# Channel order, DRAM layout and transfers of the query and key stacks in a four-layer kernel on one core

## The chip, the cores and the metric

The kernel runs on one core of one Trainium2 chip. The metric is the device time of one execution in microseconds (us), here the median of three runs. The engines are TensorE (PE), VectorE (DVE), ScalarE (ACT), GpSimd (POOL) and SyncE (SP). Every transfer in this kernel is issued by SP, and 16 DMA engines carry them.

## The reference

`x` has shape 8 x 512 x 128: eight batches of 512 tokens with 128 channels. Four layers follow each other, and each has the form `x = x + attn(xn) * act(ffn(xn))`, where `xn` is the layer norm of `x`. Layer 0 attends in a band of 32 tokens, layer 2 is linear attention. What is changed touches layers 1 and 3:

```python
# layer 1: causal attention, 8 heads of 8 channels, on the first 64 channels ("local"),
# and on 128 compressed tokens ("global")
lq, lk, lv = jnp.split(local_x @ w_lqkv + b_lqkv, 3, axis=-1)
local_out = _causal_attn(_split_heads(lq, Tx), _split_heads(lk, Tx), _split_heads(lv, Tx))
gq, gk, gv = jnp.split(cg @ w_gqkv + b_gqkv, 3, axis=-1)
# layer 3: attention without a mask, 16 heads of 8 channels, 512 tokens
q = jnp.einsum('btd,hdk->bhtk', hidden_states, Wq) + bq[None, :, None, :]
k = jnp.einsum('btd,hdk->bhtk', hidden_states, Wk) + bk[None, :, None, :]
scores = jnp.einsum('bhtk,bhsk->bhts', q, k) * scale
```

## The kernel before

**Two threads.** The work on a batch is cut in two programs. Thread A does layers 0 and 1, thread B does layers 2 and 3 with the mixtures of experts of layers 1 to 3. In turn n, thread A works on batch n and thread B on batch n-1, so turn 0 holds A alone, turns 1 to 7 hold both, and turn 8 holds B alone. Each engine executes its instructions in one fixed order. That order is woven when the program is written: each thread is a Python generator with one `yield` before each stretch of instructions, the table `STARTS` holds one number for each `yield`, and `weave` always continues the thread whose next number is lower, with `TURN` added for each further batch. The numbers only set the order of the instructions on each engine (SP's queue too). They set no time: what an engine waits for is written as semaphore waits. An engine whose next instruction waits does nothing of the other thread meanwhile.

**The stacks.** Queries and keys are computed channel by channel (`F3`, 128 partitions: 16 heads of 8 channels, and `FL`, `FG`, 64 partitions: 8 heads of 8). VectorE splits each value into three bf16 parts (`dve_split`, lines 1017 to 1020), so `SPL3` and `SPL` hold, for each channel, three parts of 512 tokens, and `SPLG` three parts of 128. A score is then a product over a stack of 72 partitions (9 pairs of a query part and a key part with 8 channels each), with 3 more partitions for ones and the row maximum. To bring 8 channels x 3 parts of every head under each other, the parts go through DRAM. `stack_out` stores them, with one transfer for each part: 3 for the queries and 5 for the keys (types 0, 1, 2, 0, 1). `stack_in` loads them as three blocks of 24 partitions, for the queries three times the same block, for the keys shifted by one type (`HD` rows) each time. So one stack takes 8 stores and 6 loads. In DRAM the order is head, type, channel, token, and each contiguous run is 512 tokens of bf16, 1 KB (256 B of it in the global part). There are three stacks for each batch: local and global in thread A (`QSL`, `KSL`, `QSG`, `KSG`) and that of layer 3 in thread B (`QS3`, `KS3`).

**What follows the stacks.** In thread B, TensorE computes 32 pairs of score tiles (line 1720), VectorE takes their maxima (line 1568), negates and splits them (lines 1572 to 1576), TensorE turns them (line 1731), ScalarE copies them (line 1426), three small transfers put them in `QS3` (line 1327), and 64 scores are computed again the other way round (line 1753), with ScalarE's exponential (line 1434) and the products with the values (line 1742). In thread A, the same is done for layer 1 (scores in line 1194).

**What lies beside them.** While thread B is at the stack of layer 3, thread A is at the end of the band attention of layer 0: ScalarE's exponential (line 786), four stores of the weights in runs of 128 B with a skew (`band_scratch`, line 658), four loads of the bands (line 664), products with the values (line 1126), the sums of the weights (line 1134), VectorE's reciprocal and product (lines 934, 935) and the projection (line 1140). All these transfers are on SP's queue, as are the stacks' ones and the weights of the expert pairs (`WST`, `GW`).

Of the kernel before, what the change touches and what calls it, by code (L numbers as in the profile page):

```python
# [1945 lines left out]
```

## Time and profile before

| What | Value |
|---|---|
| Median of the runs | 3959.35 us (3958.97 to 3961.12) |
| The profiled execution | 3941.28 us |
| Its span, first to last instruction | 3939.5 us |
| Granted TensorE clock, mean | 0.864 |
| PE busy | 3131.8 us, 79% of the span |
| DVE busy | 2503.1 us, 64% |
| ACT busy | 1661.7 us, 42% |
| POOL busy | 689.7 us, 18% |
| DMA | 330.82 MB in 332,142 packets, mean 84 GB/s |

The profile is of one execution, which took 18.07 us less than the median. The shares are means over stages that differ much: in the stage of the stacks most engines stand idle for some 10 us, and in the expert stages TensorE is busy nearly all the time. A granted clock of 1.00 is 2.4 GHz and one of 0.50 is 1.2 GHz.

### The profile page before, as it was taken

The page shows a single profiled execution, that of the slowest core. Times are in us where ns is not written, and L with a number is a line of the kernel's source. Part 1 is how long each engine was busy: PE and PEld are TensorE (multiplying, and loading weights), DVE is VectorE, ACT ScalarE, POOL GpSimd, SP SyncE. Part 2 cuts the span into 40 slices and gives each one's busy share as a digit, 9 for nine tenths or more (in the row PEclk, how much of TensorE's full clock was granted, in tenths as well). Part 3 has the DMA queues.
Part 4 walks back from the last instruction along what each step waited for, and adds up shares of the span by engine and source line. Part 5 has one row for each costly group of instructions (what it writes and reads, how often), then busy time and mean ns, then how long its engine had stood idle before and what let it go on. Part 6 is the DMA issues. An engine that isn't in the chain of part 4 may idle for free.

```text
span 3939.5 us, 43890 instructions
## 1 busy us (share of the span) xinstructions
PE 3131.8 (79%) x16174; PEld 1566.9 (40%) x16174; DVE 2503.1 (64%) x4568; ACT 1661.7 (42%) x2458; POOL 689.7 (18%) x465
## 2 busy tenths in 40 slices
PE   4458768987799778997699868997689867996588
PEld 1124323553245333553245432553235432454145
DVE  5534876578656876669755776568765786534542
ACT  3415515464344524464154534455154643431241
POOL 2001201311023101312013110322013110211030
PEclk8568879997799879998699978998799987997696
DMA  2330174302741164301842055501743027411261
GB/s 90 36 97 31 31 133 119 105 8 79 122 138 55 23 118 122 116 16 43 144 131 76 1 106 103 157 29 32 132 121 103 7 78 122 135 57 43 58 193 48
DMA packets 332142, 330.82 MB, mean 84 GB/s; under 512 B 101448, under 2 KB 267144, under 8 KB 331656
## 3 DMA queue, kind: packets, MB, share of 16 engines
q1 hardware_dynamic: 331928, 328.01, 34.8%
q8 instruction: 128, 2.10, 0.2%
q14 instruction: 86, 0.70, 0.1%
HBM read 278.88 MB, written 47.78 MB: 83 GB/s over the span
## 4 chain that ended last, share of the span: by engine, by line
PE 55%; DVE 23%; DMA 7%; ACT 5%; SPq 4%; issue 4%; POOL 2%; ACTq 0%; DVEq 0%; POOLq 0%
PE PS L1774 6%; PE PS L1797 6%; PE PS L1628 5%; PE PS L1801 5%; PE PS L1636 5%; DMA U<-band_scratch 4%; PE PS L1075 4%; PE PS L1742 3%; DVE MX L1568 3%; SPq L658 3%; PE PS L1753 3%; DVE U L885 2%; DVE XN L558 2%; DVE U L878 2%; DVE D L1619 2%
## 5 line engine op out<-in xcount | busy, mean ns | idle before, releaser
L1380 POOL TENSOR_TENSOR D<-D,GW 128x512 f32<-128x512 f32 x320 | 429.5, 1343 | 1419.1 <-ACT D L1453 1190.9
L770 ACT ACTIVATE U<-U 128x2048 f32<-128x2048 f32 x256 | 488.7, 1909 | 188.6 <-DVE U L878 104.4
L1614 DVE SCALAR_TENSOR_TENSOR D<-D,PS 128x512 f32<-128x512 f32 x336 | 228.9, 681 | 400.9 <-ACT D L1457 283.6
L1453 ACT ACTIVATE D<-PS 128x512 f32<-128x512 f32 x336 | 200.1, 595 | 615.9 <-PE PS L1797 615.9
L1774 PEld LDWEIGHTS PS<-WST,D 128*128 128x128 f32 (+1 forms) x2688 | 350.4, 197 | 163.9 <-DVE D L1619 99.7
L1774 PE MATMUL PS<-WST,D 128*128 128x128 f32 (+1 forms) x2688 | 378.5, 285 | 31.6 <-DVE D L1619 31.5
L1801 PE MATMUL PS<-XT,WST 128*128 128x512 f32 (+1 forms) x672 | 373.4, 638 | 28.8 <-DVE D L1614 27.8
L1075 PE MATMUL PS<-U,resident 128*32 128x512 f32 x2048 | 306.1, 678 | 112.1 <-ACT U L770 112.1
L885 DVE SCALAR_TENSOR_TENSOR U<-PP,RD,QB 128x512 f32<-128x512 f32 x512 | 361.7, 771 | 46.4 <-ACT QB L767 27.6
L1568 DVE TENSOR_REDUCE MX<-PS 128x2 f32<-128x1024 f32 x256 | 299.5, 1220 | 121.9 <-PE PS L1720 121.8
L1797 PE MATMUL PS<-XT,WST 128*128 128x512 f32 (+1 forms) x672 | 366.6, 628 | 9.8 <-DMA WST<-in_pairs_dram 6.5
L1720 PE MATMUL PS<-UU 128*128 128x512 bf16 x512 | 220.8, 536 | 138.6 <-DMA UU<-k_scratch 83.2
L1434 ACT ACTIVATE D<-PS 128x512 f32<-128x512 f32 x512 | 269.0, 604 | 119.1 <-PE PS L1753 119.0
L878 DVE TENSOR_TENSOR U<-EP,QE 128x2048 f32<-128x2048 f32 x128 | 306.2, 2409 | 16.0 <-PE PS L1075 15.2
L1636 PEld LDWEIGHTS PS<-UU,D 128*128 128x128 f32 x2048 | 264.4, 191 | 121.5 <-issue 115.5
L1619 DVE TENSOR_TENSOR D<-D 128x512 f32<-128x512 f32 x336 | 252.1, 750 | 38.8 <-POOL D L1380 31.5
L1628 PE MATMUL PS<-XT,UU 128*128 128x512 f32 x512 | 269.7, 614 | 0.9 <-DVE GB L1587 0.9
L1636 PE MATMUL PS<-UU,D 128*128 128x128 f32 x2048 | 269.3, 276 | 0.0
L1393 ACT ACTIVATE D<-PS,resident 128x512 f32<-128x512 f32 x256 | 173.6, 684 | 144.6 <-PE PS L1628 144.0
L562 POOL TENSOR_TENSOR RS<-VE,half 128x4 f32<-128x4 f32 x32 | 46.1, 1441 | 993.0 <-DVE VE L554 993.0
L1753 PE MATMUL PS<-UU 128*128 128x512 bf16 x512 | 164.6, 406 | 46.1 <-DMA UU<-NMT 33.3
L1457 ACT ACTIVATE D<-PS 128x512 f32<-128x512 f32 x336 | 199.7, 594 | 0.0
(350 smaller groups left out, 4035.4 us busy)
## 6 DMA issues: line engine op xcount, KB each, us to landing
GW<-gates_scratch SPq DMA_DIRECT2D x320, 256.0 KB, 4.2
WST<-in_pairs_dram SPq DMA_DIRECT2D x336, 192.0 KB, 2.4
U<-band_scratch SPq DMA_DIRECT2D x32, 1280.0 KB, 14.9
UU<-in_w_dram SPq DMA_DIRECT2D x64, 512.0 KB, 7.4
UU<-q_scratch SPq DMA_DIRECT2D x24, 384.0 KB
UU<-k_scratch SPq DMA_DIRECT2D x24, 384.0 KB
e_scratch<-D SPq DMA_DIRECT2D x8, 1024.0 KB, 4.5
D<-e_scratch SPq DMA_DIRECT2D x32, 256.0 KB, 3.9
```

Source lines behind the costliest of these rows:

```text
L770: e.activation(ring(i), ring(i), ACT.Gelu).then_inc(S["act"], 1)
L878: last = e.tensor_tensor(ring(i).rearrange("p (q t) -> p q t", q=4), win, QE[:, h, :].unsqueeze(1).broadcast_to([P, 4, T]), ALU.add)
L885: last = e.scalar_tensor_tensor(out=ring(i)[:, T * x:T * x + T], in0=PP[:, h, PAD - o:PAD - o + T], scalar=RD[:, HOR - 1 - o:HOR - o], in1 ...
L1075: last = e.matmul(PS(L0_BANK[g, kind])[32 * q:32 * q + 32, :], wout[:, 1 - kind, c, :], ring(i)[:, T * x:T * x + T], start=(c == 0), stop= ...
L1380: e.tensor_tensor(AV[:, n % 3, :], AV[:, n % 3, :], GW[:, p // 2 % GWS, p % 2, :], ALU.mult).then_inc(S["gated"], 1)
L1568: e.tensor_reduce(MX3[:, j:j + 2, hd], PSall[:, 4 + j:6 + j, :], AX.X, ALU.max).then_inc(S["max3"], 1)
L1619: e.tensor_tensor(AV[0:m, n % 3, :], AV[0:m, n % 3, :], SL[0:m, n % 3, :], ALU.mult).then_inc(S["av"], 1)
L1628: e.matmul(PZ(f % 2), w1slot(x)[:, 0, P * f:P * f + P], XT(b), start=True, stop=True).then_inc(S["h1_ps"], 1)
L1636: last = e.matmul(PZ(2 + x % 2)[:, P * j:P * j + P], HB[:, x % 2, f, P * j:P * j + P], w1slot(x)[:, 1, P * f:P * f + P], start=(j == 0 and ...
L1774: last = e.matmul(PZ(3)[:, P * j:P * j + P], AV[0:m, n % 3, P * j:P * j + P], WST[0:m, (PAIRS * b + n) % WS, 2, :], start=(p == 0 and j == ...
L1797: e.matmul(PZ(0)[0:m, :], w[:, 0, 0:m], XT(b), start=True, stop=True).then_inc(S["u_ps"], 1)
L1801: e.matmul(PZ(1)[0:m, :], w[:, 1, 0:m], XT(b), start=True, stop=True).then_inc(S["v2_ps"], 1)
```

## The change

The channels of the queries and keys are reordered on the host from head, dimension to dimension, head (`by_dim`), in the weights and the biases. A partition of `SPL3` is then a pair of dimension and head, and the DRAM arrays become two-dimensional: a row for each type and dimension, and in the row all heads' tokens in a row, 16 KB for layer 3, 8 KB for the local stack and 2 KB for the global one. One store now writes all three parts of the queries, one the first three types of the keys, one the last two. The stacks are filled by two loads each: one for the first 48 partitions, and one for the last 24. What is stored and what stands in the stacks in the end is as many bytes as before.

```diff
-        ql_dram = nc.dram_tensor("ql_scratch", (NH // 2, 3, HD, T), BF16).ap()
+        ql_dram = nc.dram_tensor("ql_scratch", (3 * HD, NH // 2 * T), BF16).ap()
...
-        k3_dram = nc.dram_tensor("k3_scratch", (NH, 5, HD, T), BF16).ap()
+        k3_dram = nc.dram_tensor("k3_scratch", (5 * HD, NH * T), BF16).ap()
...
         def stack_out(e, spl, nh, n, qd, kd, q_sem, k_sem):
-            for k in range(3):
-                dst = bass.AP(qd.tensor, k * HD * T, [[3 * HD * T, nh], [T, HD], [1, n]])
-                e.dma_start(dst, spl[0:8 * nh, 0, k, 0:n]).then_inc(S[q_sem], 16)
-            for k in range(5):
-                dst = bass.AP(kd.tensor, k * HD * T, [[5 * HD * T, nh], [T, HD], [1, n]])
-                e.dma_start(dst, spl[0:8 * nh, 1, KTYPES[k], 0:n]).then_inc(S[k_sem], 16)
-
-        def stack_in(e, stack, rows, shift, nh, n, dram, signal):
-
-            for r in range(3):
-                e.dma_start(stack[24 * r:24 * r + 24, 0:nh, 0:n], bass.AP(dram.tensor, r * shift * T, [[T, 24], [rows * T, nh], [1, n]])).then_inc(S[signal], 16)
+            e.dma_start(bass.AP(qd.tensor, 0, [[n, 8 * nh], [8 * nh * n, 3], [1, n]]), spl[0:8 * nh, 0, :, 0:n]).then_inc(S[q_sem], 16)
+            for k0, k1 in ((0, 3), (3, 5)):
+                dst = bass.AP(kd.tensor, k0 * 8 * nh * n, [[n, 8 * nh], [8 * nh * n, k1 - k0], [1, n]])
+                e.dma_start(dst, spl[0:8 * nh, 1, 0:k1 - k0, 0:n]).then_inc(S[k_sem], 16)
+
+        def stack_in(e, stack, shift, nh, n, dram, signal):
+
+            for r0, r1 in ((0, 2), (2, 3)):
+                src = bass.AP(dram.tensor, r0 * shift * nh * n, [[shift * nh * n, r1 - r0], [nh * n, 24], [1, nh * n]])
+                e.dma_start(stack[24 * r0:24 * r1, 0:nh * n], src).then_inc(S[signal], 16)
```

The first pair in an access pattern is its slowest dimension: a step and a count. The waits follow the numbers of transfers (`q_out3` from 48 to 16, `k_out3` from 80 to 32, `stacked3` from 96 to 64, and so on).

Second, chains of VectorE instructions get a `yield` between their steps, so that the other thread's instructions may come in between: `dve_split`, `dve_kept`, `dve_gates`, `dve_update`, the splitting of the maxima, parts of layer 2 and of the mixing. The instructions are the same but for one: the reciprocal of line 934 is cut into two of 512 elements.

```diff
             e.wait_ge(S["den"], at("den", b, 1))
-            step(e, e.reciprocal(RCA[:, :, :], PSall[:, 2:4, :]))
+            for h in range(2):
+                last = e.reciprocal(RCA[:, h, :], PS(2 + h))
+                if h == 0:
+                    yield
+            step(e, last)
+            yield
             e.tensor_tensor(OS[:, :, :], OS[:, :, :], RCA[:, :, :], ALU.mult).then_inc(S["on"], 1)
...
         def dve_split(e, f, part, signal):
             step(e, e.tensor_copy(part(0), f))
+            yield
             step(e, e.tensor_tensor(f, f, part(0), ALU.subtract))
+            yield
             step(e, e.tensor_copy(part(1), f))
+            yield
             e.tensor_tensor(part(2), f, part(1), ALU.subtract).then_inc(S[signal], 1)
```

Third, `TURN` and all of `STARTS` are new. The lines of the table in which the end of the band attention meets thread B's scores:

```diff
-TURN = 429.40
+TURN = 423.40
...
     "a_dve": (
-        181.59, 182.54, 184.12, 188.61, 192.04, 194.85, 209.94, 212.88, 264.22, 274.87, 275.50, 277.88, 280.62, 287.54, 291.47, 300.89,
+        179.49, 180.44, 182.02, 186.51, 189.93, 190.58, 192.75, 192.97, 207.85, 210.79, 262.47, 262.91, 263.47, 266.13, 266.76, 267.63,
...
     "a_pe": (
-        183.40, 183.46, 184.85, 186.75, 198.54, 211.08, 213.25, 214.20, 215.14, 216.09, 244.09, 249.11, 254.26, 259.70, 262.09, 272.76,
+        181.30, 181.35, 182.74, 184.63, 196.45, 208.98, 209.93, 210.88, 211.83, 212.78, 242.37, 247.34, 252.30, 258.11, 260.34, 264.02,
...
     "b_pe": (
-        264.01, 268.48, 268.73, 268.97, 269.61, 270.11, 270.60, 271.10, 272.05, 272.29, 272.52, 274.66, 274.89, 275.84, 276.08, 276.32,
+        259.55, 265.92, 266.17, 266.41, 267.05, 267.55, 268.04, 268.54, 269.49, 269.73, 269.96, 270.58, 271.08, 272.03, 272.27, 272.50,
```

Which `yield` a number belongs to follows from the code. In `a_pe` the last six numbers of the line are the four band products (line 1126), the sums (line 1134) and the projection (line 1140). In `b_pe` the first two are the transposes of the maxima (line 1731) and the first score of line 1753; the last of the 32 score pairs (line 1720) stands at 260.65 before and at 253.49 after. In `a_dve`, 264.22 is the reciprocal with its product and 274.87 the addition behind the projection before; after, these are 262.47 and 262.91 (the two reciprocals), 263.47 (the product) and 266.13.

## Rows read from the trace of the kernel before

**Rows 1.** The page, section 4: the chain that ended last, by line.

```profile
PE PS L1774 6%; PE PS L1797 6%; PE PS L1628 5%; PE PS L1801 5%; PE PS L1636 5%; DMA U<-band_scratch 4%; PE PS L1075 4%; PE PS L1742 3%; DVE MX L1568 3%; SPq L658 3%; PE PS L1753 3%; DVE U L885 2%; DVE XN L558 2%; DVE U L878 2%; DVE D L1619 2%
```

**Rows 2.** Timeline of SyncE: start us, length us, where X is saved in turns 1 and 7.

```profile
510.17 0.33 SPq L1311 DMA_DIRECT2D x_scratch<-X  x1
...
3227.39 0.33 SPq L1311 DMA_DIRECT2D x_scratch<-X  x1
```

**Rows 3.** Timeline of SyncE in turn 4: start us, length us, issue.

```profile
1881.52 1.85 SPq L702 DMA_DIRECT2D q_scratch<-D  x3
...
1886.63 1.57 SPq L710 DMA_DIRECT2D UU<-q_scratch  x3
...
1893.40 17.35 SPq L658 DMA_DIRECT2D band_scratch<-D  x4
1910.79 20.36 SPq L664 DMA_DIRECT2D U<-band_scratch  x4
...
1979.54 1.96 SPq L702 DMA_DIRECT2D ql_scratch<-D  x3
```

**Rows 4.** Timeline of TensorE in turn 4: start us, length us; in brackets the idle time before.

```profile
1903.76 1.89 PE L1720 MATMUL PS<-UU 128*128 128x512 bf16 x4 [8.53 <-DMA UU<-k_scratch]
...
1927.22 2.36 PE L1126 MATMUL PS<-U,VP 128*32 128x160 f32 x32 [1.23 <-DMA U<-band_scratch]
...
1944.76 1.08 PE L1126 MATMUL PS<-U,VP 128*32 128x128 f32 x32
...
1947.08 1.96 PE L1134 MATMUL PS<-QE,consts 128*128 128x512 f32 x4
1951.69 0.40 PE L1731 MATMUL PS<-identb,NM 128*48 128x128 bf16 x4 [2.65 <-DVE NM L1576]
1956.19 2.94 PE L1753 MATMUL PS<-UU 128*128 128x512 bf16 x6 [4.10 <-DMA UU<-NMT]
...
1961.34 1.95 PE L1140 MATMUL PS<-resident,QE 128*128 128x128 f32 x16
...
2004.08 0.22 PE L1194 MATMUL PS<-U 128*128 128x128 bf16 x1
```

**Rows 5.** Timeline of VectorE in turn 4.

```profile
1904.84 22.43 DVE L1568 TENSOR_REDUCE MX<-PS 128x2 f32<-128x1024 f32 x19 [11.28 <-PE PS L1720]
...
1941.81 5.83 DVE L1568 TENSOR_REDUCE MX<-PS 128x2 f32<-128x1024 f32 x5 [0.20 <-PE PS L1720]
...
1951.55 6.55 DVE L934 RECIPROCAL D<-PS 128x1024 f32<-128x1024 f32 x1
1958.13 1.23 DVE L935 TENSOR_TENSOR QE<-QE,D 128x1024 f32<-128x1024 f32 x1
```

**Rows 6.** Timeline of SyncE in turn 8, where thread B runs alone.

```profile
3646.32 1.87 SPq L702 DMA_DIRECT2D q_scratch<-D  x3
...
3652.27 1.57 SPq L710 DMA_DIRECT2D UU<-q_scratch  x3
```

**Rows 7.** Timeline of TensorE in turn 8.

```profile
3668.51 1.89 PE L1720 MATMUL PS<-UU 128*128 128x512 bf16 x4 [24.32 <-DMA UU<-k_scratch]
```

**Rows 8.** Timeline of VectorE in turn 8.

```profile
3669.58 37.40 DVE L1568 TENSOR_REDUCE MX<-PS 128x2 f32<-128x1024 f32 x32 [12.84 <-PE PS L1720]
```

**Rows 9.** Windows: stretch, length, busy us by engine, TensorE clock, DMA share, GB/s.

```profile
3660.00:3662.00 2.00, 0.00 (x0) 0.00 (x0) 0.00 (x0) 0.00 (x0) 0.00 (x0) 0.50 0.83 169
...
252.00:253.00 1.00, 1.00 (x2) 0.34 (x1) 0.00 (x0) 0.58 (x1) 0.00 (x0) 0.50 0.40 102
...
3635.00:3636.00 1.00, 0.00 (x0) 0.00 (x0) 0.96 (x4) 0.00 (x0) 0.00 (x0) 0.50 0.10 19
...
2019.00:2021.00 2.00, 0.77 (x5) 0.25 (x3) 2.00 (x2) 1.08 (x2) 1.00 (x1) 1.00 1.03 410
```

**Rows 10.** Timeline of SyncE in turn 0, where thread A runs alone.

```profile
250.66 1.89 SPq L702 DMA_DIRECT2D ql_scratch<-D  x3
```

**Rows 11.** Timeline of TensorE in turn 0.

```profile
265.05 0.29 PE L1194 MATMUL PS<-U 128*128 128x128 bf16 x1 [3.99 <-DMA U<-kl_scratch]
```

More of the change, by code:

```diff
@@ L91, in laid_out, with by_dim @@
     beside = lambda v, n: np.asarray(v).reshape(n, P, -1).transpose(1, 0, 2).reshape(P, -1)
+    def by_dim(w):
+        w = np.asarray(w)
+        return w.reshape(w.shape[:-1] + (-1, HD)).swapaxes(-1, -2).reshape(w.shape)
     def per_head(w):
@@ L112, in laid_out @@
     bc[:, 36:38] = w("L0_attn_b_disp").reshape(2, P).T
-    bc[:, 38] = w("L3_attn_bq").reshape(-1)
-    bc[:, 39] = w("L3_attn_bk").reshape(-1)
+    bc[:, 38] = by_dim(w("L3_attn_bq").reshape(-1))
+    bc[:, 39] = by_dim(w("L3_attn_bk").reshape(-1))
     for k, n in ((40, "L1_attn_b_lqkv"), (42, "L1_attn_b_gqkv")):
-        bc[0:LD, k] = w(n)[0:LD]
-        bc[0:LD, k + 1] = w(n)[LD:2 * LD]
+        bc[0:LD, k] = by_dim(w(n)[0:LD])
+        bc[0:LD, k + 1] = by_dim(w(n)[LD:2 * LD])
     bc[0:LD, 44] = w("L1_attn_b_comp")[LD:C]
@@ L131, in laid_out @@
     v["lu"] = w("L0_ffn_lora_up").transpose(0, 2, 1).reshape(P, C)
-    v["wqkv1"] = np.concatenate([w("L1_attn_w_lqkv"), w("L1_attn_w_gqkv")], 1)
+    v["wqkv1"] = np.concatenate([f(w(n)[:, LD * k:LD * k + LD]) for n in ("L1_attn_w_lqkv", "L1_attn_w_gqkv")
+                                 for k, f in enumerate((by_dim, by_dim, np.asarray))], 1)
     v["wcomp"] = beside(w("L1_attn_w_comp"), R1).reshape(P, R1, C)[:, :, LD:].reshape(P, -1)
@@ L141, in laid_out @@
     v["b_out"] = rows(w("L2_attn_b_out"))
-    v["wqkv3"] = np.concatenate([w(f"L3_attn_{n}").transpose(1, 0, 2).reshape(C, P) for n in ("Wq", "Wk", "Wv")], 1)
+    v["wqkv3"] = np.concatenate([w(f"L3_attn_{n}").transpose(1, *o).reshape(C, P) for n, o in (("Wq", (2, 0)), ("Wk", (2, 0)), ("Wv", (0, 2)))], 1)
     v["bv"], v["gate_bias"] = rows(w("L3_attn_bv")), rows(w("L3_ffn_gate_bias"))
@@ L285 @@
     "band_used": 4, "f0_ps": 4, "f0_sb": 2, "a_f": 1, "a_t": 1, "a_x": 1, "a_best_dif": 2, "a_best_exp": 2,
-    "qk_ps": 2, "qk": 4, "v_ps": 2, "v": 2, "split": 2, "q_out": 48, "k_out": 80, "split_out_g": 128, "stacked": 96, "stacked_g": 96,
+    "qk_ps": 2, "qk": 4, "v_ps": 2, "v": 2, "split": 2, "q_out": 16, "k_out": 32, "split_out_g": 48, "stacked": 64, "stacked_g": 64,
     "zero_a": 3, "ones_a": 32, "s1": 40, "max": 40, "nm": 1, "nm_t": 1, "nmt": 1, "nm_in": 96, "s2": 40, "p": 40, "pv": 10,
@@ L672, in a_sp @@
             yield
[L673 to L674 removed]
+            e.wait_ge(S["q_out"], at("q_out", b, 16))
+            stack_in(e, UB[:, 0:8 * T], 0, 8, T, ql_dram, "stacked")
             yield
[L676 to L677 removed]
+            e.wait_ge(S["k_out"], at("k_out", b, 32))
+            stack_in(e, UB[:, 8 * T:16 * T], HD, 8, T, kl_dram, "stacked")
             yield
@@ L917, in a_dve @@
             dve_best(e, A8[:, 1], A8[:, 0], A8[:, 2], A8[:, 3], 1, 1, 8, 2, "a_best_dif")
-            dve_kept(e, A8[:, 1], A8[:, 0], A8[:, 2], 1, 1, 8, 2)
+            yield from dve_kept(e, A8[:, 1], A8[:, 0], A8[:, 2], 1, 1, 8, 2)
             yield
             e.wait_ge(S["a_best_exp"], at("a_best_exp", b, 1))
-            step(e, dve_gates(e, A8[:, 3], A8[:, 2], A8[:, 4], AS, 1, 1, 8))
+            step(e, (yield from dve_gates(e, A8[:, 3], A8[:, 2], A8[:, 4], AS, 1, 1, 8)))
             e.tensor_copy(GX[0:1, :].rearrange("p (e r) -> p e r", e=8), A8[0:1, 4, 0, 0:8].unsqueeze(2).broadcast_to([1, 8, 16])).then_inc(S["f0_sb"], 1)
@@ L933, in a_dve @@
             e.wait_ge(S["den"], at("den", b, 1))
-            step(e, e.reciprocal(RCA[:, :, :], PSall[:, 2:4, :]))
+            for h in range(2):
[3 more added lines that the diff above has]
+            step(e, last)
+            yield
             e.tensor_tensor(OS[:, :, :], OS[:, :, :], RCA[:, :, :], ALU.mult).then_inc(S["on"], 1)
@@ L940, in a_dve @@
             e.wait_ge(S["a_t"], at("a_t", b, 1))
-            dve_update(e, b, 0.5).then_inc(S["a_x"], 1)
+            (yield from dve_update(e, b, 0.5)).then_inc(S["a_x"], 1)
             e.wait_ge(S["a_x"], at("a_x", b, 1))
@@ L945, in a_dve @@
             e.wait_ge(S["qk"], at("qk", b, 2))
-            dve_split(e, FL[0:64, :, :], lambda k: SPL[0:64, :, k, :], "split")
+            yield from dve_split(e, FL[0:64, :, :], lambda k: SPL[0:64, :, k, :], "split")
             yield
@@ L951, in a_dve @@
             e.wait_ge(S["qk"], at("qk", b, 4))
-            dve_split(e, FG[0:64, :, 0:P], lambda k: SPLG[0:64, :, k, :], "split")
+            yield from dve_split(e, FG[0:64, :, 0:P], lambda k: SPLG[0:64, :, k, :], "split")
             yield
@@ L960, in a_dve @@
             dve_best(e, A8[:, 1], A8[:, 0], A8[:, 2], A8[:, 3], P, NT, E1, 2, "a_best_dif")
-            dve_kept(e, A8[:, 1], A8[:, 0], A8[:, 2], P, NT, E1, 2)
+            yield
+            yield from dve_kept(e, A8[:, 1], A8[:, 0], A8[:, 2], P, NT, E1, 2)
             yield
             e.wait_ge(S["a_best_exp"], at("a_best_exp", b, 2))
-            dve_gates(e, A8[:, 3], A8[:, 2], GT1(b), AS, P, NT, E1).then_inc(S["g1"], 1)
+            (yield from dve_gates(e, A8[:, 3], A8[:, 2], GT1(b), AS, P, NT, E1)).then_inc(S["g1"], 1)
             e.wait_ge(S["g1"], at("g1", b, 2))
@@ L978, in a_dve @@
             step(e, last)
+            yield
             for v in both:
@@ L984, in a_dve @@
             step(e, last)
+            yield
             for v in both:
@@ L993, in a_dve @@
             e.reciprocal(RCA[:, 1, 0:P], PS(1)[:, 0:P])
+            yield
             step(e, e.reciprocal(RCA[:, 0, :], PS(0)))
+            yield
             each = lambda v: v.unsqueeze(2).broadcast_to([P, P, R1])
@@ L1003, in a_dve @@
             e.wait_ge(S["mix"], at("mix", b, 2))
+            yield
             step(e, e.tensor_tensor(SB(b), LO(b), over(WDIF[:, 0:C]), ALU.mult))
+            yield
             step(e, e.tensor_reduce(AS[:, :], SB(b), AX.X, ALU.add))
@@ L1017, in dve_split @@
             step(e, e.tensor_copy(part(0), f))
+            yield
             step(e, e.tensor_tensor(f, f, part(0), ALU.subtract))
+            yield
             step(e, e.tensor_copy(part(1), f))
+            yield
             e.tensor_tensor(part(2), f, part(1), ALU.subtract).then_inc(S[signal], 1)
@@ L1476, in b_dve @@
             e.wait_ge(S["b_t"], at("b_t", b, 1))
-            dve_update(e, b, 0.5).then_inc(S["b_x"], 1)
+            (yield from dve_update(e, b, 0.5)).then_inc(S["b_x"], 1)
             e.wait_ge(S["b_x"], at("b_x", b, 1))
@@ L1483, in b_dve @@
             step(e, e.tensor_scalar(KV[:, :, 0, :], ps[:, :, 0, :], 0.0, EPS2, ALU.max, ALU.add))
+            yield
             e.tensor_copy(KV[:, :, 1, :], ps[:, :, 1, :]).then_inc(S["l2_dve"], 1)
+            yield
             e.tensor_scalar(HT(b), PZ(1), 0.0, EPS2, ALU.max, ALU.add).then_inc(S["l2_dve"], 1)
@@ L1501, in b_dve @@
             step(e, e.reciprocal(SM[:, :], SM[:, :]))
+            yield
             for j in range(NT):
@@ L1504, in b_dve @@
             last.then_inc(S["l2_dve"], 1)
-            dve_kept(e, SCO, M8, RPL, P, NT, E2, K2)
+            yield
+            yield from dve_kept(e, SCO, M8, RPL, P, NT, E2, K2)
             yield
@@ L1508, in b_dve @@
             e.wait_ge(S["gate_act"], at("gate_act", b, 1))
-            dve_gates(e, DIF, RPL, GT, SM, P, NT, E2).then_inc(S["gate_dve"], 1)
+            (yield from dve_gates(e, DIF, RPL, GT, SM, P, NT, E2)).then_inc(S["gate_dve"], 1)
             yield from b_dve_pairs(e, b, 2)
@@ L1514, in b_dve @@
             e.wait_ge(S["b_t"], at("b_t", b, 2))
-            dve_update(e, b, 1.0).then_inc(S["b_x"], 1)
+            (yield from dve_update(e, b, 1.0)).then_inc(S["b_x"], 1)
             e.wait_ge(S["b_x"], at("b_x", b, 2))
@@ L1519, in b_dve @@
             e.wait_ge(S["qk3"], at("qk3", b, 2))
-            dve_split(e, F3[:, :, :], lambda k: SPL3[:, :, k, :], "split3")
+            yield from dve_split(e, F3[:, :, :], lambda k: SPL3[:, :, k, :], "split3")
             yield
@@ L1572, in b_dve @@
             step(e, e.tensor_scalar(f, MX3[:, :, :], -1.0, None, ALU.mult))
+            yield
             step(e, e.tensor_copy(part(0), f))
             step(e, e.tensor_tensor(f, f, part(0), ALU.subtract))
+            yield
             step(e, e.tensor_copy(part(1), f))
@@ L1602, in b_dve_pairs @@
                     e.tensor_tensor(OS3[:, :, :], OS3[:, :, :], RC, ALU.mult).then_inc(S["nrm3"], 1)
+                    yield
                     e.wait_ge(S["nrm3"], at("nrm3", b, 3))
```

39 lines of the change are left out of this document (17 added, 22 removed), and 167 rows, old and new, of tables (PER, STARTS).

## The prediction

> **What bounds the kernel now.** I read the page first, then the chain of waits, then the timelines engine by engine around the stacks. The chain runs through many lines with single-digit shares, most of them TensorE's, but `U<-band_scratch` (DMA) and line 658 (SP's queue) stand among them with 4% and 3% [rows 1]. So the kernel is a sequence of stages with different limits. A joint turn lasts (3227.39 - 510.17) / 6 = 452.9 us [rows 2], and there are seven of them.
>
> The stage in question, in turn 4: the first store of the stack of layer 3 is issued at 1881.52, the first load at 1886.63, and then SP waits for the band weights and stores them from 1893.40 [rows 3]. TensorE starts the scores at 1903.76, after 8.53 us of waiting for the key load [rows 4], so 22.2 us lie between first store and first score. Then VectorE's maxima set the pace, from 1904.84 to 1941.81 + 5.83 = 1947.64, or 42.8 us [rows 5]. Band products stand between them and wait for their loads (1927.22 to 1944.76, the first and the last of four) [rows 4]. The reader is to see that two chains run side by side here, the stack with its maxima and the bands, and that both must end before line 1753 starts at 1956.19. In turn 8 the stack is alone: 3646.32 to 3668.51 is again 22.2 us [rows 6, 7], and the 32 maxima take only 37.40 [rows 8].
>
> **The loads.** What a DMA reaches depends on how many of the 16 engines carry it. The windows show it [rows 9]: a store whose slow dimension on the DRAM side is 8 (local stack) keeps a share of 0.40 busy. The loads with 24 partitions stand at 0.83, with 169 GB/s, long after the last was issued. The fill of three partitions shows 0.10 and 19 GB/s. Loads over 128 partitions reach 1.03 and 410 GB/s. The share follows the smaller of the counts in the slowest dimension, and 0.83 against 1.03 is some 12 or 13 of 16 engines. In the new load of 48 partitions the source's slowest dimension has a count of 2. By this series it runs on two engines, and the 24-row load on as many as now.
>
> The Trainium skill says the same as a rule (DMA: Bandwidth & Descriptors, "Why a DMA increments its semaphore by 16 and not by 1"): the number of engines is the largest up to 16 that divides the slowest counts of both sides. For 48 against 2 it gives 2, and for 24 it gives 12; the shares above agree. The same page's "Rules for kernel authors" advises joining small transfers into large ones, which speaks for this change; the sum below goes by the shares.
>
> Rate of one engine: 410 / (16 x 1.03) = 24.9 GB/s with long runs. The other end is today's stack load, 169 / 12 = 14.1 GB/s with 1 KB runs. I take 24.9, because runs grow to 16 KB and two engines fall short of today's total by far.
>
> Layer 3, each of queries and keys: 48 rows of 16,384 B over two engines are 24 x 16,384 / 24.9 = 15.8 us; the third block, two rows for each of 12 engines, adds 1.3. Together 2 x 17.1 = 34.2 us. The first load is issued 5.1 us after the first store now [rows 3]; with one store for the queries that is between one issue (0.6) and 5.1, and I take 4. Start and landing add 2.2: in turn 8 the six loads, 2.36 MB at 169 GB/s or 14.0 us, took 3668.51 - 3652.27 = 16.2. First store to first score: 4 + 34.2 + 2.2 = 40.4 us against 22.2, so **+18.2 us**. At 14.1 GB/s it would be +44. On 16 engines the loads would take 2.36 MB / 398 GB/s = 5.9, in all 12.1, so -10.1.
>
> **Turn 8:** no cover, +18.2. **Turn 0:** the local stack, 250.66 to 265.05, takes 14.4 us [rows 10, 11]. After: 4 + 2 x (24 x 8,192 B / 24.9 = 7.9, and 0.7) + 2.2 = 23.4, so +9.0.
>
> **Joint turns, layer 3.** Scores start at 1881.52 + 40.4 = 1921.9. The bands: engines 0 and 1 are free at about first store + 38; the band stores took 17.4 us and the loads 20.4 [rows 3], so the first band is there at about + 60 and the last at + 77. The new table puts the first band behind about 23 score pairs, at 40.4 + 27 = 67, and the last two behind all of them, at 78: just hidden. The maxima then end at 1921.9 + 1.1 + 37.4 = 1960.4 against 1947.64: **+12.8 us**, as the band waits (5.4 us) fall away.
>
> **Joint turns, the table.** Before, the sums (line 1134) run ahead of the transposes (line 1731), and the reciprocal fills the time in which the maxima travel [rows 4, 5]. The new table has transposes 259.55, sums 260.34, projection 264.02, first score 265.92. Between the first reciprocal and the addition behind the projection it leaves 266.13 - 262.47 = 3.7 us, where the row has 6.55 for the reciprocal alone [rows 5]. TensorE keeps its order, so the first score of line 1753 now waits for sums 1.96, reciprocals 6.55, product about 1.2 and projection 1.95: 0.6 + 1.96 + 6.55 + 1.3 + 1.95 = 12.4 us after the maxima are split, against 1956.19 - 1951.6 = 4.6 now. Of these 7.8 us, 1.95 is work that leaves the later stretch. **+5.8 us.** Behind it stand all of thread B's scores, ScalarE's exponentials and the expert pairs.
>
> **Joint turns, local stack.** From projection to thread A's first score are 42.7 us now, without a wait [rows 4]; the table cuts this distance from 39.46 to 35.95, or about 38.9 in real time. The chain needs 1979.54 - 1961.34 = 18.2 to the first store [rows 3, 4], and then 23.4: 41.6. **+2 us**, between 0 and 5. The global stack (2 KB runs) is needed 24 us later in the table and lands in time.
>
> **What costs nothing or helps a little.** The `yield`s add no instruction. Two reciprocals in place of one add at most 0.1 us. Eight issues of about 0.6 us each become three; SP waits for the band weights until 1893.40 anyway [rows 3], so that frees nothing there. The channel order changes no matmul shape. `TURN` is 6.0 us shorter, and of that the two steps above are just what the plan got wrong; I credit 1 us for the rest, between 0 and 6.
>
> **The sum.** 7 x (12.8 + 5.8 + 2 - 1) = 137.2, and with 18.2 + 9.0 it is 164.4. Profiled execution: 3941.3 + 164.4 = 4105.7; the median of before lies 18.1 above its profiled one, so **4124 us**, 4% slower.
>
> **Rivals.** (1) *The loads spread over 12 or more engines after all* (the other side). For it: the transfers of the other lines with long runs reach 410 GB/s [rows 9]. Against it: every row whose slow count is below 16. Turn 8 gains between 2.0 us (4 + 14.0 + 2.2, the loads as fast as now) and 10.1, turn 0 about 3. In joint turns the scores start early, but the last band at 1944.76 stands ahead of the transposes, then sums, reciprocal, product and projection: first score at about 1958.8 instead of 1956.2, less 1.95. So nothing is won there but what the rest of the table gives, 1 to 5 us. Time 3959 - 10 - 7 x 2 = 3935, range 3915 to 3951. It decides when the loads do their 94.8 us of engine time (2.36 MB at 24.9 GB/s) in less than 22.2 - 6.2 = 16.0 us, that is from 6 engines on.
>
> (2) *Two engines, at the slow rate or with the bands behind them.* The band transfers queue behind the stack on engines 0 and 1; if they take 10 us longer than I allow, or an engine gives 14 GB/s, each turn loses 10 to 30 us more: 4240 and above.
>
> (3) *Two engines, but hidden.* If the table's order leaves TensorE other work and the reciprocals fall under the late scores, only turn 8, turn 0 and some us of each turn stay: 3967 to 3990.
>
> **Chances and range.** Forecast (3990 to 4240): 0.75. Rival 2: 0.03. Rival 3: 0.05. No change, gains and the table's stall in balance: 0.05. Rival 1: 0.12. The range 3967 to 4240 holds the forecast and rival 3, 0.80. A measurement of this kernel can tell about 0.2% (8 us) from no change: slower 0.83, same 0.05, faster 0.12.
>
> **What would show it.** In the windows between the last stack load and the first score the DMA share should fall to about 2/16 = 0.12 with some 50 GB/s, where it is 0.83 and 169 now. Line 1720's wait for the key load in turn 8 should grow from 24.3 to about 42 us, and in joint turns the scores should start some 40 us after the first store. Line 1140 should show a wait for line 935 of some 8 us, and line 1753 should come behind it. In turn 0, line 1194 should wait about 12 us for the local stack, instead of 3.99. The prediction is wrong if these windows show a share above 0.5, if the band loads end far beyond the scores, or if the expert stages shift by themselves.

## The result and the profile after

The changed kernel takes 4119.46 us in the median of four runs (4116.41 to 4121.84), where the kernel before takes 3959.16 on the same chip. The ratio is 1.0401, 95% interval 1.0385 to 1.0418: 4% slower, 160.3 us by the medians. The prediction said 4124. The profiled execution took 4121.84 us, with a span of 4120.1 and a mean granted clock of 0.847.

The page, section 4, the chain that ended last, by engine and by line (after):

```profile
PE 46%; DVE 24%; DMA 14%; ACT 5%; issue 3%; another core or an unknown queue 3%; POOL 2%; SPq 2%; ACTq 0%; DVEq 0%; POOLq 0%
DMA UU<-k_scratch 7%; DVE MX L1597 6%; PE PS L1806 6%; PE PS L1829 6%; PE PS L1833 5%; PE PS L1660 5%; PE PS L1668 4%; DMA U<-kl_scratch 3%; PE PS L1100 3%; DVE U L888 3%; DVE U L895 2%; PE PS L1774 2%; DVE XN L565 2%; POOL D L1405 2%
```

The lines to compare with [rows 1] are the loads of the key stacks. Before, neither was among the lines shown there: the chain waited for each only once, for `UU<-k_scratch` 13.5 us in turn 8 and for `U<-kl_scratch` 7.0 us in turn 0. Now `UU<-k_scratch` (layer 3) leads it with 7%, and `U<-kl_scratch` (local) has 3%. The packets fell only from 332,142 to 296,780.

**Turn 8, the stack alone.** Two windows (after): in the first the last load is issued, at 3816.21, and in the second only the loads are left. The last three figures are granted clock, DMA share, GB/s:

```profile
3815.00:3820.00 5.00, 0.00 (x0) 0.00 (x0) 4.62 (x32) 0.00 (x0) 0.00 (x0) 0.50 0.58 124
3820.00:3830.00 10.00, 0.00 (x0) 0.00 (x0) 0.62 (x3) 0.00 (x0) 0.00 (x0) 0.50 0.12 50
```

In the second window and those behind it the share is 0.12 to 0.13, two engines of sixteen, where [rows 9] has 0.83 and 169 GB/s. That is 25 to 27 GB/s for each engine. The timeline of SyncE, turn 8 (after):

```profile
3810.27 0.37 SPq L711 DMA_DIRECT2D q_scratch<-D  x1
...
3816.21 1.09 SPq L720 DMA_DIRECT2D UU<-k_scratch  x2
```

and that of TensorE with its first score (after):

```profile
3851.50 1.49 PE L1752 MATMUL PS<-UU 128*128 128x512 bf16 x3 [43.28 <-DMA UU<-k_scratch]
```

From the first store to the first score are 3851.50 - 3810.27 = 41.2 us, where [rows 6, 7] give 22.2 and the prediction said 40.4. The waits, summed over the run (after; us in total, times, longest):

```profile
PE PS L1752 <- DMA UU<-k_scratch: 240.0, 8, 43.3
...
PE PS L1219 <- DMA U<-kl_scratch: 26.0, 8, 12.1
```

The first was 83.2 us in 8 with a longest of 24.3 before. The second is new but for turn 0, where it was 3.99 and is now 12.1.

**Turn 4, a joint turn.** The timeline of SyncE (after), which answers to [rows 3]:

```profile
1959.06 0.39 SPq L711 DMA_DIRECT2D q_scratch<-D  x1
...
1962.21 1.13 SPq L720 DMA_DIRECT2D UU<-q_scratch  x2
...
1970.94 35.95 SPq L669 DMA_DIRECT2D band_scratch<-D  x4
2006.94 21.14 SPq L675 DMA_DIRECT2D U<-band_scratch  x4
...
2075.52 0.61 SPq L711 DMA_DIRECT2D ql_scratch<-D  x1
```

The stores of the band weights take 35.95 us to issue, where they took 17.35. TensorE, the same turn (after), which answers to [rows 4]:

```profile
2000.35 1.49 PE L1752 MATMUL PS<-UU 128*128 128x512 bf16 x3 [28.41 <-DMA UU<-k_scratch]
...
2026.30 1.29 PE L1151 MATMUL PS<-U,VP 128*32 128x160 f32 x32
...
2038.22 1.08 PE L1151 MATMUL PS<-U,VP 128*32 128x128 f32 x32
2043.31 0.62 PE L1763 MATMUL PS<-identb,NM 128*48 128x128 bf16 x4 [4.00 <-DVE NM L1607]
2043.86 3.78 PE L1159 MATMUL PS<-QE,consts 128*128 128x512 f32 x4
2055.56 3.79 PE L1165 MATMUL PS<-resident,QE 128*128 128x128 f32 x16 [7.92 <-DVE QE L950]
2059.57 0.65 PE L1785 MATMUL PS<-UU 128*128 128x512 bf16 x2 [0.22 <-issue]
...
2098.61 0.23 PE L1219 MATMUL PS<-U 128*128 128x128 bf16 x1 [2.02 <-DMA U<-kl_scratch]
```

VectorE, the same turn (after), which answers to [rows 5]:

```profile
2001.02 26.95 DVE L1597 TENSOR_REDUCE MX<-PS 128x2 f32<-128x1024 f32 x23 [29.91 <-PE PS L1752]
...
2037.81 1.23 DVE L1597 TENSOR_REDUCE MX<-PS 128x2 f32<-128x1024 f32 x1 [0.20 <-PE PS L1752]
...
2043.03 0.23 DVE L1607 TENSOR_TENSOR NM<-NMF,NM 128x64 bf16<-128x64 f32 x1
2047.68 6.57 DVE L945 RECIPROCAL D<-PS 128x512 f32<-128x512 f32 x2 [4.42 <-PE PS L1159]
2054.28 1.23 DVE L950 TENSOR_TENSOR QE<-QE,D 128x1024 f32<-128x1024 f32 x1
```

Read together: the scores start 41.3 us after the first store (22.2 before), the maxima end at 80.0 (66.1 before), the maxima are split at 84.2 (70.1). Then TensorE makes the sums, waits 7.92 us for VectorE's reciprocal and product, makes the projection and only then starts line 1785, which was line 1753 before, at 100.5 (74.7 before). Thread A's first score follows at 139.6 (122.6 before).

The turns, from where X is saved in turn 1 to turn 7 (after, SyncE), beside [rows 2]:

```profile
518.05 0.33 SPq L1336 DMA_DIRECT2D x_scratch<-X  x1
...
3370.74 0.33 SPq L1336 DMA_DIRECT2D x_scratch<-X  x1
```

(3370.74 - 518.05) / 6 = 475.4 us for a joint turn, 22.6 more than before.

### The profile page after: what moved, and what is told of

It reads as the page before. It is cut to its first block, busy times and chain, and to the rows that moved or that the text cites. A ratio compares the mean times of both kernels' runs of the same rounds, so it can differ in the third digit from the quotient of the medians.

```text
span 4120.1 us, 43645 instructions
## 1 busy us (share of the span) xinstructions
PE 3107.6 (75%) x16089; PEld 1576.7 (38%) x16174; DVE 2504.3 (61%) x4576; ACT 1662.0 (40%) x2458; POOL 692.7 (17%) x465
## 4 chain that ended last, share of the span: by engine, by line
PE 46%; DVE 24%; DMA 14%; ACT 5%; issue 3%; another core or an unknown queue 3%; POOL 2%; SPq 2%; ACTq 0%; DVEq 0%; POOLq 0%
DMA UU<-k_scratch 7%; DVE MX L1597 6%; PE PS L1806 6%; PE PS L1829 6%; PE PS L1833 5%; PE PS L1660 5%; PE PS L1668 4%; DMA U<-kl_scratch 3%; PE PS L1100 3%; DVE U L888 3%; DVE U L895 2%; PE PS L1774 2%; DVE XN L565 2%; POOL D L1405 2%
## 5 line engine op out<-in xcount | busy, mean ns | idle before, releaser
L1752 PE MATMUL PS<-UU 128*128 128x512 bf16 x489 | 210.9, 529 | 302.9 <-DMA UU<-k_scratch 240.0
L1478 ACT ACTIVATE D<-PS 128x512 f32<-128x512 f32 x336 | 200.2, 596 | 579.9 <-PE PS L1829 579.1
L1459 ACT ACTIVATE D<-PS 128x512 f32<-128x512 f32 x512 | 270.4, 602 | 202.6 <-remote 116.8
L1752 PEld LDWEIGHTS PS<-UU 128*128 128x128 bf16 x512 | 33.4, 106 | 474.1 <-DMA UU<-k_scratch 238.8
```

What stands on the lines that cost most here:

```text
L1459: e.activation(PT3[:, k % 8, :], PZ(k % 3), ACT.Exp, scale=SCALE).then_inc(S["p3"], 1)
```

## Experiments on the loads

Each kernel has its ratio to the kernel before, timed beside it on the same chip. The kernel before took 3959.16 us beside the changed one, but 3976.72 to 3983.38 beside the experiments. So only ratios are compared across these groups, and, between profiles, the time since the first store of the stack. Microseconds for a difference of ratios are worked out on 3959.

**Three loads of 24 rows** (`e1_three_loads`): the change with only the joining of the first two blocks undone.

```diff
-            for r0, r1 in ((0, 2), (2, 3)):
+            for r0, r1 in ((0, 1), (1, 2), (2, 3)):
```

> The changed kernel with each stack filled by three loads of 24 rows instead of one of 48 and one of 24; rows stay 16, 8 and 2 KB, the table stays the new one. Theory 1 (a load runs on as many engines as its smaller slowest count allows): 24 rows run on about 12 engines, so 2.36 MB take some 8 us, first store to first score in turn 8 falls from 41.2 to 14 to 16 us, the DMA share meanwhile rises above 0.5, and the time falls by 130 to 180 us, to 3940 to 3990. Theory 2 (long rows into few partitions are slow by themselves, whatever the number of engines): the time stays within 20 us of 4119. Theory 3 (the new table is the cause): it stays too.

Measured: 3950.09 us against 3983.38, ratio 0.9916 (0.9891 to 0.994). One line (and the counts of the waits that go with it) makes 0.8% faster out of 4% slower, which is 192 us, a little more than the 130 to 180 expected. So the joined load is the cause of the loss. The first score was expected 14 to 16 us after the first store, and that was too early: it comes at 19.8. A window in turn 8 while the loads run (three loads):

```profile
3676.00:3680.00 4.00, 0.00 (x0) 0.00 (x0) 2.75 (x14) 0.00 (x0) 0.00 (x0) 0.50 0.68 147
```

TensorE's first score there, with the first store at 3668.56:

```profile
3688.33 1.89 PE L1752 MATMUL PS<-UU 128*128 128x512 bf16 x4 [21.71 <-DMA UU<-k_scratch]
```

In turn 4, SyncE issues the band stores in 16.79 us again, as before (three loads):

```profile
1899.34 0.38 SPq L711 DMA_DIRECT2D q_scratch<-D  x1
...
1911.23 16.79 SPq L669 DMA_DIRECT2D band_scratch<-D  x4
1928.07 23.67 SPq L675 DMA_DIRECT2D U<-band_scratch  x4
```

So the long issue of the band stores follows from the stack's loads. In turn 4 it ends 28.7 us after the first store here and 47.8 us in the change, and the first scores stand at 20.1 and 41.3: in every variant it ends 6 to 9 us after the first score. Whether SyncE is held up by the small number of engines, or only until the loads are through, these runs don't separate.

**One load of 72 rows** (`e8_one_load`): the slowest dimension of the source then has a count of 3.

```diff
-            for r0, r1 in ((0, 2), (2, 3)):
+            for r0, r1 in ((0, 3),):
```

> The changed kernel with one load of 72 rows per stack operand, whose source has a slowest count of 3. Theory 1: three engines of 24 rows each work side by side, DMA share about 3/16 = 0.19, 75 to 80 GB/s, and each operand takes 15.1 to 15.8 us instead of 17, so turn 8 gains about 3 us and the time falls by 10 to 30 us, to 4090 to 4110. Theory 2: the share stays at 0.12 and the time within 8 us of 4119, or it rises.

Measured: 4053.19 us, ratio 1.0176 (1.0153 to 1.0198). A window of turn 8 (one load):

```profile
3757.00:3762.00 5.00, 0.00 (x0) 0.00 (x0) 0.00 (x0) 0.00 (x0) 0.00 (x0) 0.50 0.18 79
```

A share of 0.18 is three engines, at 26 GB/s each, and the first score comes 34.7 us after the first store. The count was right and the size was not: against 1.0401 this gives back 2.2%, some 90 us, where I had expected 10 to 30. The first score gains 6.5 us in turn 8, where 3 were expected, and the gain grows on the way through a joint turn. In turn 4 the scores start 6.1 us earlier (35.2), the maxima end 6.0 earlier (74.0), line 1785 starts 11.0 earlier (89.5) and thread A's first score comes 12.8 earlier (126.8). Part of this is peculiar to that turn. The change (after), one step in the splitting of the maxima and GpSimd beside it:

```profile
2039.79 3.20 DVE L1606 CAST NM<-NMF 128x64 bf16<-128x64 f32 x1
...
2039.40 3.55 POOL L738 MEMSET U<- 128x4096 f32 x1 [92.56 <-PE PS L1151]
```

The same with one load, and TensorE behind it:

```profile
2005.48 0.20 DVE L1606 CAST NM<-NMF 128x64 bf16<-128x64 f32 x1
...
2005.63 3.51 POOL L738 MEMSET U<- 128x4096 f32 x1 [87.43 <-PE PS L1151]
...
2005.99 0.40 PE L1763 MATMUL PS<-identb,NM 128*48 128x128 bf16 x4 [0.45 <-DVE NM L1607]
2006.77 1.95 PE L1159 MATMUL PS<-QE,consts 128*128 128x512 f32 x4 [0.38 <-ACT QE L802]
```

In the change GpSimd's memset of line 738 started just ahead of the cast, and the cast ended 0.04 us after the memset. Here the cast came first and took 0.20 us. So TensorE waited 0.45 us for the maxima instead of 4.00, and ran the sums in 1.95 us instead of 3.78. In turns 1, 3, 6 and 7 the cast is slow here too (3.2 to 3.4 us), and line 1785 gains only 4.8 to 7.0 us. Averaged over the seven joint turns the maxima end 5.6 us earlier, thread A's first score comes 9.3 earlier, and a turn is 10 shorter. Of the 9.3, 2.0 are the wait for the local stack, which is gone in the joint turns: only turn 0 still waits for it, 9.5 us, where the change has 26.0 us in eight.

**48 contiguous rows** (`e2_flat48`): the DRAM arrays repeat the types (six for the queries, seven for the keys), so that the first load is 48 rows in one piece and both its slowest counts are 48. It costs two more stores.

```diff
...
-                src = bass.AP(dram.tensor, r0 * shift * nh * n, [[shift * nh * n, r1 - r0], [nh * n, 24], [1, nh * n]])
+                src = bass.AP(dram.tensor, (0 if r0 == 0 else 4 * shift) * nh * n, [[nh * n, rows], [1, nh * n]])
```

> The changed kernel with the DRAM arrays lengthened to 6 types of queries (0 1 2 0 1 2) and 7 of keys (0 1 2 1 2 0 1), so that the first 48 partitions are loaded from 48 rows that lie one after another: the same two loads per operand, the same rows of 16 KB, but a slowest count of 48 on both sides instead of 48 against 2. Five stores instead of three, 0.64 MB more. New table. Theory 1 (engines by slowest count): 16 and 12 engines, first store to first score 15 to 21 us instead of 41.2, time 3930 to 3990 where before is 3983. If the limit of about 165 GB/s that 24 rows on 12 engines show is one of the 24 target partitions, 48 partitions run near twice that and the score starts at 16 to 17 us; if it is one of these reads as a whole, at 20 to 21 us. Theory 2 (one load of 48 partitions with long rows is slow by itself): within 20 us of the changed kernel, 1.04 of before.

Measured: 3954.82 us against 3978.89, ratio 0.9936 (0.9915 to 0.9958). A window of turn 8 (48 contiguous rows):

```profile
3673.00:3677.00 4.00, 0.00 (x0) 0.00 (x0) 1.87 (x7) 0.00 (x0) 0.00 (x0) 0.50 0.91 143
```

The large transfer is harmless once its slowest count is 48: joining as such was not at fault. But 14 to 16 busy engines carry no more than twelve, 168 GB/s (in the window 3677 to 3683). The score comes at 22.1, no earlier than before, and a little behind the 20 to 21 that I expected if the reads as a whole are limited. With a limit set by the 24 target partitions it would have come at 16 to 17, so 48 partitions did not lift the limit. Part of the 22.1 are the two more stores: the first load is issued 3.9 us after the first store, with three loads 2.5. Against three loads, 0.9936 and 0.9916 are not apart beyond their intervals.

**Six and four rows** (`e10_six_rows`, `e11_four_rows`): the stack in 12 loads of 6 rows, or 18 of 4.

```diff
-            for r0, r1 in ((0, 2), (2, 3)):
...
+            for j in range(12):
+                src = bass.AP(dram.tensor, (j // 4 * shift + j % 4 * 6) * nh * n, [[nh * n, 6], [1, nh * n]])
+                e.dma_start(stack[6 * j:6 * j + 6, 0:nh * n], src).then_inc(S[signal], 16)
```

> The changed kernel with each stack loaded by twelve transfers of 6 rows (slow count 6 on both sides) instead of 48 + 24 rows. Engines follow the smaller slow count: 6 engines at the 26 to 28 GB/s that an engine showed when 2 or 3 carried the loads are 156 to 168 GB/s, which is what 12 engines reached (165). So the first score of the layer-3 stack comes 20 to 22 us after the first store, as with loads of 24 rows, 1 to 2 us later for 24 issues in place of 6; the loss is gone, 0.99 to 1.00 of before. If each engine gives only the 14 GB/s that it showed among 12, the loads take 28 us, the score comes at 34 and the kernel stands at 1.015 or above.

> The same with eighteen transfers of 4 rows. Engine-bound, 4 x 26 to 28 = 104 to 112 GB/s: 2.36 MB take 21 to 23 us, the first score comes 27 to 29 us after the first store (41.3 with two engines, 35.2 with three, 20.1 with twelve), and the kernel stands between those of three and twelve engines, 1.00 to 1.01 of before. At 14 GB/s for each engine it would be 42 us and the whole loss of the changed kernel, 1.04.

Measured: 3984.17 us (3965.49 to 4004.21 in ten runs) with six rows, ratio 1.0019 (1.0 to 1.0038), and 4022.95 with four, ratio 1.0104 (1.0076 to 1.0132). Windows of turn 8 (six rows):

```profile
3689.00:3693.00 4.00, 0.00 (x0) 0.00 (x0) 0.00 (x0) 0.00 (x0) 0.00 (x0) 0.50 0.37 98
3693.00:3697.00 4.00, 0.00 (x0) 0.00 (x0) 0.00 (x0) 0.00 (x0) 0.00 (x0) 0.50 0.40 109
```

and one with four rows:

```profile
3735.00:3740.00 5.00, 0.00 (x0) 0.00 (x0) 0.00 (x0) 0.00 (x0) 0.00 (x0) 0.50 0.27 108
```

The shares are right, 0.26 for four engines and 0.36 to 0.40 for six. The rates are not: four engines give 26 to 27 GB/s each, six only 16 to 18. Over the turns the first score comes 26 to 29 us after the first store with six rows, and 30 to 35 with four, later than the 20 to 22 and 27 to 29 that I expected, and both ratios lie at or just above the upper end of what I gave (1.00 and 1.01). So there is a second limit. Of all the variants, by the windows of turn 8:

| Slowest count | DMA share | GB/s | First store to first score, turn 8, us | Ratio to before |
|---|---|---|---|---|
| 2 (48 + 24 rows, the change) | 0.12 to 0.13 | 50 to 54 | 41.2 | 1.0401 |
| 3 (72 rows) | 0.18 | 79 | 34.7 | 1.0176 |
| 4 (4 rows) | 0.26 to 0.27 | 108 | 31.1 | 1.0104 |
| 6 (6 rows) | 0.36 to 0.40 | 98 to 109 | 29.4 | 1.0019 |
| 24 (24 rows) | 0.68 to 0.76 | 147 to 164 | 19.8 | 0.9916 |
| 48 and 24 | 0.89 | 168 | 22.1 | 0.9936 |

Up to four engines the engines are the limit, 25 to 27 GB/s each. Beyond, the engines are no longer the limit: six carry no more than four, and from twelve on the total ends near 165. What holds it there these runs don't show.

## Experiments on the table

**The new layout with the old table** (`e3_old_table`): the kernel before with the channel order, the DRAM layout, three stores and two-engine loads, but with the old `STARTS` and none of the added `yield`s.

```diff
     "a_pe": (
...
-        181.30, 181.35, 182.74, 184.63, 196.45, 208.98, 209.93, 210.88, 211.83, 212.78, 242.37, 247.34, 252.30, 258.11, 260.34, 264.02,
+        183.40, 183.46, 184.85, 186.75, 198.54, 211.08, 213.25, 214.20, 215.14, 216.09, 244.09, 249.11, 254.26, 259.70, 262.09, 272.76,
```

> The kernel before with the new channel order, DRAM layout, three stores and two loads per stack operand, but with the old table and without the new yields and the cut reciprocal. Theory 1: the loads alone cost their part, 7 x (12.8 + 2) + 18.2 + 9.0 = 131 us at most, so 4050 to 4090, and the first score of line 1753 comes 4 to 5 us after the maxima are split, as before. Theory 3: with the old table the time is that of before, 3959 within 15.

Measured: 4128.4 us against 3983.38, ratio 1.0369 (1.0353 to 1.0385). The loads alone make nearly the whole loss. My range of 4050 to 4090, 1.023 to 1.033 of 3959, was too low. VectorE's last maxima and TensorE's line 1758 (1785 in the change) in turn 4, with the first store at 1968.30 (old table):

```profile
2048.30 5.83 DVE L1573 TENSOR_REDUCE MX<-PS 128x2 f32<-128x1024 f32 x5 [0.20 <-PE PS L1725]
...
2062.90 2.94 PE L1758 MATMUL PS<-UU 128*128 128x512 bf16 x6 [4.10 <-DMA UU<-NMT]
```

The maxima end 85.8 us after the first store, 19.7 later than before and not 12.8: that smaller figure holds only in the new table's order (13.9 in the change). Line 1758 starts at 94.6, 4.8 us after the split, as expected. So the old table loses more at the maxima and less behind them (the change stands at 80.0 and 100.5), and a joint turn takes 475.6 us against 475.4.

**The same with loads of 24 rows** (`e5_old_table_three`), `e1_three_loads`'s edit on top.

> The kernel before with the new channel order and DRAM layout, three stores, and three loads of 24 rows (about 12 engines), old table, no new yields: what the change could have been. Theory 1: the score starts 2.4 us earlier than before as in the three-load run (19.8 instead of 22.2), the bands are as before, so each joint turn and turn 8 gain 0 to 2.5 us: 0.994 to 1.000 of before. Beside the three-load run with the new table (0.9916) it says what the new table and the yields are worth by themselves: 0 to 0.8%. A theory that the new table costs by itself (its stall of some 8 us in each joint turn not paid back) wants this run below 0.985.

Measured: 3956.97 us against 3978.89, ratio 0.9951 (0.9933 to 0.9969). So layout and fewer stores are worth 0.5% by themselves, and the new table another 0.35% (0.9916), which is just clear of the noise. Both lie in what I expected. The joined load with the old table costs the difference to 1.0369, 4.2%.

**Two slots of TensorE's table moved** (`e4_proj_slot`): the sums go ahead of the transposes of the maxima, and the projection behind the first scores of line 1785, as both stood before.

```diff
-        ... 242.37, 247.34, 252.30, 258.11, 260.34, 264.02,
+        ... 242.37, 247.34, 252.30, 258.11, 258.80, 270.20,
```

> The changed kernel with two numbers of the table moved: the sums (line 1159 of the changed kernel) stand at 258.80, ahead of the transposes of the maxima, and the projection at 270.20, behind the first scores of thread B, as in the old table. The loads stay on two engines. If the projection in front of the scores costs what the trace shows (16.3 us instead of 4.6 from split maxima to first score, less the projection's own 3.8), the time falls by 7 x 6 to 7 x 9 = 42 to 63 us, to 4056 to 4077. If that stretch is covered by other work, it stays within 10 us of 4119.

Measured: 4116.17 us against 3983.38, ratio 1.0331 (1.0314 to 1.0348), 0.7% under the 1.0401 of the change, or 28 us, where I had expected 42 to 63. TensorE in turn 4 (two slots moved):

```profile
2043.17 1.08 PE L1151 MATMUL PS<-U,VP 128*32 128x128 f32 x32
2045.49 1.95 PE L1159 MATMUL PS<-QE,consts 128*128 128x512 f32 x4 [1.24 <-ACT QE L802]
2048.25 0.40 PE L1763 MATMUL PS<-identb,NM 128*48 128x128 bf16 x4 [0.81 <-DVE NM L1607]
2052.76 2.94 PE L1785 MATMUL PS<-UU 128*128 128x512 bf16 x6 [4.10 <-DMA UU<-NMT]
...
2058.30 1.95 PE L1165 MATMUL PS<-resident,QE 128*128 128x128 f32 x16
```

The wait for the reciprocal is gone, and line 1785 starts at 88.8 us after the first store instead of 100.5. Yet thread A's first score comes at 137.2 instead of 139.6: the projection itself has only moved from 96.5 to 94.3, because the last band product came no earlier, and thread A's stack follows it at a distance of 43 us in both. The stall stood ahead of thread B's scores, but the chain of thread A lay beside it, and its timing fits that it took most of the gain.

**Both repairs** (`e6_three_slot`): the two slots moved, and loads of 24 rows.

> Three loads of 24 rows, new table, with the sums ahead of the transposes (258.80) and the projection behind the first scores (270.20). The two-engine pair of runs gave 0.7% for this move (1.0401 to 1.0331). If the stall of the projection is a cost of its own, it is worth 0.5 to 0.9% here too: 0.983 to 0.987 of before. If late stacks and this stall only add where both are there, it stays at 0.9916.

Measured: 3933.15 us against 3978.89, ratio 0.9883 (0.9862 to 0.9903). It is the fastest of all, 1.2% faster than before. The move is worth 0.33% here (0.9916 to 0.9883), less than the 0.5 to 0.9% expected: in turn 4 line 1785 starts at 71.2 us instead of 82.2, but thread A's first score only at 118.0 instead of 119.5.

**The same with 48 contiguous rows** (`e7_flat_slot`).

> 48 rows that lie one after another (16 engines), new table with the two slots moved. Both gains together: 0.5 to 0.9% below the run with 48 rows and the table as it is.

Measured: 3948.37 us against 3978.89, ratio 0.9923 (0.9905 to 0.9942). The move gains 0.13% here (0.9936 to 0.9923), which can't be told from nothing, where 0.5 to 0.9% was expected. And 48 rows, with their two more stores, are 0.4% behind 24 (0.9883), this time beyond the noise.

## Why the prediction was right

**Loads on two engines: right, and shown.** Share, rate (25 to 27 GB/s for each engine against the 24.9 assumed), the first score in turn 8 (41.2 against 40.4) and the local stack in turn 0 (273.08 - 250.13 = 22.95 us against 23.4) came as worked out. In turn 8 two small errors met: the first load is issued 2.5 us after the first store and not 4, and from there the scores start 38.7 us later and not 36.4. The rule in the Trainium skill (DMA: Bandwidth & Descriptors, "Why a DMA increments its semaphore by 16 and not by 1") agrees closely with the shares at counts of 2, 3, 4 and 6 (0.12 to 0.40), and roughly at 24 (0.68 to 0.76 for twelve engines) and 48 (0.89). The advice of the same page of the Trainium skill ("Rules for kernel authors") to join small transfers did not hold for the loads with slowest counts of 2 and 3 (1.0401 and 1.0176), and brought nothing measurable for that with 48 (0.9936 against 0.9916). With three stores in place of eight and the number of loads unchanged the kernel was 0.5% faster (0.9951), but the layout changed with it.

**Joint turns, layer 3: right.** The first band product came 67.2 us after the first store (67 predicted) and the last at 79.2 (78). The maxima ended 80.0 - 66.1 = 13.9 us later, against 12.8 predicted. The number needs the new table, though: with the old one it was 19.7.

**The table's stall: right in its mechanism, mis-sized in two ways.** From the split of the maxima to line 1785 it took 2059.57 - 2043.26 = 16.3 us, not 12.4. Sums and projection last 3.78 us each and not 1.95. The windows of turn 4 show why (after; the granted clock stands third from the end):

```profile
2043.00:2048.00 5.00, 4.33 (x8) 1.54 (x8) 0.55 (x2) 0.59 (x1) 1.77 (x2) 0.50 0.09 22
2048.00:2055.50 7.50, 0.00 (x0) 0.00 (x0) 7.46 (x3) 0.00 (x0) 0.00 (x0) 0.50 0.70 180
```

TensorE had waited 4.00 us for the split maxima, and runs these groups at 0.50, half the full clock. Where they stand ahead of the transposes, at the end of a busy stretch, the clock is 1.00 (two slots moved):

```profile
2045.00:2048.00 3.00, 1.95 (x4) 0.68 (x4) 2.96 (x2) 0.34 (x1) 3.00 (x2) 1.00 0.00 0
```
On the other side, most of the stall does not reach the end of the turn. At its place it measures 16.3 - 4.6 = 11.7 us, but the moved slots give back 28 / 7 = 4 us per joint turn; 5.8 were predicted. Table and `yield`s together cost 0.3% with two-engine loads (1.0369 to 1.0401), some 13 us, where the sum has 7 x (5.8 - 1) = 34, and gain 0.35% with twelve engines (0.9951 to 0.9916). If the stall costs 4 us per turn, the rest of the new table gives some 2 and not the 1 that I credited.

Part of the delay behind the maxima was there before the change as well: beside GpSimd's memsets (lines 728 to 730 before, 738 to 740 after) the splitting took some 3 us longer in each joint turn, in the kernel before, in the change and with the slots moved (one step of 3.20 us in the change, three of 1.82, 0.90 and 0.65 in turn 4 before, where a step takes 0.20 otherwise). No run moved it.

**Local stack: right.** The wait is 26.0 us in eight turns, of which turn 0 has 12.1, so 2.0 in each joint turn, as predicted.

**The sum: near, with errors that nearly cancel.** Joint turns grew by 22.6 us instead of 19.6, and the profiled span by 4120.1 - 3939.5 = 180.6 us instead of 164.4. But the profiled execution of before lay 18.1 us under its median, and that of after 2.4 above its own. I had carried the 18.1 over. By the medians the change is 160.3 us. The terms cancel too: by the ratios the loads alone (`e3_old_table`) cost 146 us, layout and stores included, where the sum has at most 131, and the table adds 13 where the sum has 34. That 4124 and 4119 are so close is in part luck.

**Rival 1, seen through `e1_three_loads`.** Its price, 3935 for 3959 or 0.994, was about right (0.9916), and so was its gain in turn 8 (2.4 us for 2.0). Two of its bounds fell: sixteen engines don't bring the first score at 12.1 us but at 22.1 (with two more stores), and the rival does not decide from six engines on. With six the kernel is level with before, and with twelve it is faster. **Rivals 2 and 3** are out: an engine gave 26 GB/s and not 14, and the delay stood in every turn.

## What to carry to other kernels

Before small transfers are joined, look at the slowest dimension of both sides of the new access pattern, for its count says how many DMA engines carry it; here a pattern of 2 x 24 rows was slower than two of 24, although its runs were 16 KB. The DMA share in a window without other transfers shows this at once, since 0.12 is two engines of sixteen. And price a stall by what follows it on each of the parallel chains: 5.6 us at the maxima became 9.3 at the end of the stage when later waits shrank with it, and 11.7 us in front of thread B's scores were worth only 4 where the chain of thread A stood beside them.
